# A time-mix layer with its feed-forward on one core: a sum and a root change places, values are split in two, and one half's GELU sums go to TensorE unfolded

## What is computed

```python
xk = x + xx * (time_maa_k + mk)                  # as xw, xv, xr, xg; xx = x_prev - x
r, k, v = xr @ Wr.T, xk @ Wk.T, xv @ Wv.T
g = jax.nn.silu(xg @ Wg.T)
w = time_decay + jnp.tanh(xw @ td_w1) @ td_w2;  decay = jnp.exp(-jnp.exp(w))
def step(S, inp):                                # over time, per head
    kv = k_t[..., :, None] * v_t[..., None, :]
    y = jnp.einsum('bhk,bhkj->bhj', r_t, S + u[None, :, :, None] * kv)
    S = d_t[..., None] * S + kv
...
x = _layernorm(x + attention(x))
h = jnp.einsum('btd,hd->bth', x, absmean(W_fc))  # absmean: weights to -1, 0, 1
h = layernorm(jax.nn.gelu(h, approximate=False), ln_w, ln_b)
x = _layernorm(x + jnp.einsum('bth,dh->btd', h, absmean(W_proj)))
```

## Time and profile before

| | |
|---|---|
| median of 3 runs | 3215.41 us |
| lowest and highest | 3205.75 and 3225.23 us |
| profiled execution, its time | 3207.57 us |
| its span, first to last instruction | 3205.8 us |
| PE busy | 2944.2 us, 92% |
| DVE busy | 2516.8 us, 79% |
| ACT busy | 1978.0 us, 62% |
| POOL busy | 914.2 us, 29% |
| mean granted TensorE clock | 0.981 |

### The profile page before, as it was taken

One profiled execution on the slowest core, in us unless ns is written; L12 is line 12 of the kernel. 1 busy time (PEld: TensorE's weight loads), 2 busy tenths in 40 slices (PEclk: granted clock), 3 DMA queues, 4 the chain that ended last, 5 costly groups with the idle time before them and its releaser, 6 DMA issues.

```text
span 3205.8 us, 101790 instructions
## 1 busy us (share of the span) xinstructions
PE 2944.2 (92%) x40249; PEld 2168.0 (68%) x40249; DVE 2516.8 (79%) x5336; ACT 1978.0 (62%) x4175; POOL 914.2 (29%) x793
## 2 busy tenths in 40 slices
PE   1889999999999999999999999999999999999997
PEld 0666677767676767666766766767666776666765
DVE  8467887777788778788777787777788777788787
ACT  0456667656566666667666666666567655567664
POOL 3223222223322233322232322133322222322132
PEclk9899999999999999999999999999999999999999
DMA  5000000000000000000000000000000000000000
GB/s 206 13 9 22 12 22 19 22 15 22 15 19 19 22 15 22 22 12 21 19 22 15 22 12 19 21 18 19 22 12 22 19 22 15 22 12 22 19 22 14
DMA packets 22822, 73.40 MB, mean 23 GB/s; under 512 B 3104, under 2 KB 3360, under 8 KB 20768
## 3 DMA queue, kind: packets, MB, share of 16 engines
q1 hardware_dynamic: 22432, 67.10, 6.2%
HBM read 50.31 MB, written 16.78 MB: 21 GB/s over the span
## 4 chain that ended last, share of the span: by engine, by line
PE 43%; issue 24%; DVE 14%; POOL 14%; ACT 2%; POOLq 1%; DMA 1%; DVEq 1%; SPq 0%; ACTq 0%
PE psP L404 18%; POOL MT L907 9%; PE psP L442 7%; PE psF L638 5%; PE psF L657 2%; POOL ARENA L921 2%; PE psW L498 2%; DVE ARENA L1220 2%; DVE ARENA L1168 2%; DVE SUMS L1335 2%; DVE HLO L1343 2%; DVE ARENA L1179 2%; PE psW L481 1%; POOL ARENA L943 1%; PE psY L535 1%
## 5 line engine op out<-in xcount | busy, mean ns | idle before, releaser
L404 PE MATMUL psP<-ARENA,WALL 128*128 128x256 f32 x3072 | 732.5, 396 | 66.2 <-POOL ARENA L921 64.8
L687 ACT ACTIVATE ARENA<-ARENA 32x512 f32<-32x512 f32 (+3 forms) x1026 | 584.7, 570 | 225.1 <-DVE ARENA L1168 119.3
L404 PEld LDWEIGHTS psP<-ARENA,WALL 128*128 128x128 f32 x3072 | 596.9, 198 | 154.9 <-ACT ARENA L730 67.4
L1343 DVE SCALAR_TENSOR_TENSOR HLO<-GG,FWB,HHI 128x128 f16<-128x128 f32 x1024 | 350.2, 403 | 319.2 <-ACT HHI L858 314.2
L638 PE MATMUL psF<-XLO,WFC 128*128 128x128 f16 x4096 | 489.8, 220 | 11.0 <-issue 11.0
L638 PE MATMUL psF<-XHI,WFC 128*128 128x128 f16 x4096 | 491.1, 220 | 2.7 <-DVE ST L1361 1.9
L907 POOL TENSOR_TENSOR MT<-ARENA 32x256 fp32r<-32x256 f32 x330 | 318.5, 965 | 500.6 <-ACT ARENA L687 472.0
L638 PEld LDWEIGHTS psF<-XHI,WFC 128*128 128x128 f16 x4096 | 399.2, 98 | 39.5 <-issue 33.8
L638 PEld LDWEIGHTS psF<-XLO,WFC 128*128 128x128 f16 x4096 | 402.4, 98 | 30.7 <-issue 23.0
L921 POOL TENSOR_TENSOR ARENA<-ARENA,XT 128x1024 f32<-128x1024 f32 x128 | 278.2, 2173 | 475.6 <-DVE ARENA L1102 475.6
L657 PE MATMUL psF<-WPJ,HHI 128*128 128x512 f16 x1024 | 389.7, 381 | 13.6 <-ACT GG L849 13.6
(11 more groups left out here) (166 smaller groups left out, 5234.0 us busy)
## 6 DMA issues: line engine op xcount, KB each, us to landing
XT<-x_ch SPq DMA_DIRECT2D x33, 520.0 KB, 3.4
ARENA<-x_tok SPq DMA_DIRECT2D x32, 512.0 KB, 3.7
out<-OUT SPq DMA_DIRECT2D x64, 256.0 KB, 2.1
WALL<-w_all SPq DMA_DIRECT2D x5, 1024.0 KB, 15.3
ARENA<-wfc SPq DMA_DIRECT2D x4, 1024.0 KB, 7.9
ARENA<-wpj SPq DMA_DIRECT2D x3, 1024.0 KB, 14.6
GG<-wpj SPq DMA_DIRECT2D x1, 1024.0 KB, 18.6
OUT<-w2a SPq DMA_DIRECT2D x8, 64.0 KB, 14.0
```

The lines of the kernel that those rows point to most:

```text
L404: mm = pe.matmul(psP[:, P.bank(f"{name}{g}"), COLS * c:COLS * (c + 1)], WALL[:, w, k, 128 * (2 * g + c):128 * (2 * g + c + 1)], cc(XF[slot ...
L687: return act.activation(o, i, ACT.Copy)
L1343: e = dve.scalar_tensor_tensor(out=HLO[:, k, :], in0=GG[:, u % 2, 0, 128 * m:128 * (m + 1)], scalar=FWB[:, 0, k:k + 1], in1=HHI[:, k, :], ...
```

## The change

- The row root of tile `it` leaves the end of POOL's tile and becomes `row_root(it)`, called in the next tile behind the keys' sum; the wait for `mv_ready` goes with it.
- DVE's folds of the first half go. PE sums that half from `SUMS`, four matmuls that accumulate for each of the two sums, in place of one from `GR`. Its wait is on the third addition, and DVE's first addition of the second half waits for PE's sums. The second half is folded as before.
- PE takes `up(1, 2)` between `values(0)` and `values(1)`, not behind both.
- DVE weighs the output before it updates the state.
- In the setup all eight comparisons are DVE's.

```diff
@@ PE, tile
                 values(0)
+                if ffn:
+                    ffn.up(1, 2)
                 values(1)
-                if ffn:
-                    ffn.up(1, 2)
@@ PE, feed_forward
                 def stats(j, p):
-                    pe.wait_ge(sums_folded, 2 * (PAIRS * j + p) + 2)
+                    if p:
+                        pe.wait_ge(sums_folded, 2 * (j + 1))
+                    else:
+                        pe.wait_ge(sums_added, 3 * PAIRS * j + 3)
                     F.wait_free(pe, j, f"st_{p}", first)
                     for i in range(2):
-                        mm = pe.matmul(psF[:, F.bank(f"st_{p}"), i:i + 1], GR[:, i, :], ONES[:, 0:1], start=True, stop=True)
+                        if p:
+                            mm = pe.matmul(psF[:, F.bank(f"st_{p}"), i:i + 1], GR[:, i, :], ONES[:, 0:1], start=True, stop=True)
+                        else:
+                            for m in range(4):
+                                mm = pe.matmul(psF[:, F.bank(f"st_{p}"), i:i + 1], SUMS[:, i, 128 * m:128 * (m + 1)], ONES[:, 0:1],
+                                               start=(m == 0), stop=(m == 3))
@@ POOL
-            pool.wait_ge(setup_step, 9)
-            for n, k in enumerate(POOL_PARTS):
...
                     pool.tensor_tensor(v, v, xcur, ALU.add).then_inc(xf_ready, 1)
+                    if f == 1 and not first:
+                        row_root(it - 1)
...
                 mix_low(it, 2, 10)
-                pool.wait_ge(mv_ready, 2 * (it + 1))
+
+            def row_root(t):
+
+                pool.wait_ge(mv_ready, 2 * (t + 1))
                 inverse_root(RSTD[:, :]).then_inc(rstd_ready, 1)
...
                 def alone():
+                    row_root(j)
@@ DVE, setup
-                if k in POOL_PARTS:
-                    dve.wait_ge(below_ready, POOL_PARTS.index(k) + 1)
-                else:
-                    if k:
-                        dve.wait_ge(quantised, k)
-                    dve.tensor_scalar(BELOW[0], RAW[k], SC[:, 20 + i:21 + i], None, ALU.is_lt).then_inc(setup_step, 1)
...
+                if k:
+                    dve.wait_ge(quantised, k)
+                dve.tensor_scalar(BELOW, RAW[k], SC[:, 20 + i:21 + i], None, ALU.is_lt).then_inc(setup_step, 1)
...
@@ DVE, tile
-                    if ffn and n == 4:
-                        ffn.fold(0, 0)
-                if ffn:
-                    ffn.fold(0, 1)
                 scale_left(5, 32)
...
-                state(0)
-                state(1)
                 dve.wait_ge(y_squared, 2 * it + 2)
...
                 e.then_inc(y_weighed, 1)
+                state(0)
+                state(1)
                 dve.wait_ge(p_full, P.full(it, "var"))
@@ DVE, feed_forward
                     if g == 1:
-                        if p or not first:
-                            dve.wait_ge(sums_folded, 2 * (PAIRS * j + p))
+                        if p:
+                            dve.wait_ge(f_full, F.full(j, "st_0"))
+                        elif not first:
+                            dve.wait_ge(sums_folded, 2 * j)
...
-                        stats(p)
+                        if p:
+                            fold(j, 1, 0)
+                            fold(j, 1, 1)
```

More of the change, by code:

```diff
@@ L187, in rwkv_ffn_kernel @@
         VHI, VLO = sb("VHI", [128, 2, MH], F16), sb("VLO", [128, 2, MH], F16)
-        BELOW = [h[:, :, :].rearrange("p m t -> p (m t)") for h in (HHI, HLO)]
+        BELOW = HHI[:, :, :].rearrange("p m t -> p (m t)")
         PAUSE = sb("PAUSE", [1, 8])
@@ L205, in rwkv_ffn_kernel @@
         raw_in = [sem(f"raw_in{k}") for k in range(8)]
-        below_ready = sem("below_ready")
         xt_in, xtok_in, out_stored = sem("xt_in"), sem("xtok_in"), sem("out_stored")
@@ L266, in rwkv_ffn_kernel @@
         NWEIGHTS = 8 + 5 * 4
-        POOL_PARTS = (2, 5, 7)
         def over_tiles(eng, attention, feed_forward):
@@ L571, in tile @@
                 values(0)
-                values(1)
                 if ffn:
                     ffn.up(1, 2)
+                values(1)
                 pe.wait_ge(y_squared, 2 * it + 2)
@@ L1050, in _ @@
                 part = slice(2048 * (k % 4), 2048 * (k % 4 + 1))
-                if k in POOL_PARTS:
-                    dve.wait_ge(below_ready, POOL_PARTS.index(k) + 1)
-                else:
-                    if k:
-                        dve.wait_ge(quantised, k)
-                    dve.tensor_scalar(BELOW[0], RAW[k], SC[:, 20 + i:21 + i], None, ALU.is_lt).then_inc(setup_step, 1)
-                    n += 1
-                    dve.wait_ge(setup_step, n)
+                if k:
+                    dve.wait_ge(quantised, k)
+                dve.tensor_scalar(BELOW, RAW[k], SC[:, 20 + i:21 + i], None, ALU.is_lt).then_inc(setup_step, 1)
+                n += 1
+                dve.wait_ge(setup_step, n)
                 dve.scalar_tensor_tensor(out=dst[:, :, :].rearrange("p a n -> p (a n)")[:, part], in0=RAW[k],
-                                         scalar=SC[:, 18 + i:19 + i], in1=BELOW[k in POOL_PARTS], op0=ALU.is_gt,
+                                         scalar=SC[:, 18 + i:19 + i], in1=BELOW, op0=ALU.is_gt,
                                          op1=ALU.subtract).then_inc(quantised, 1)
@@ L1351, in fold @@
                     dve.tensor_reduce(GR[:, i, :], SUMS[:, i, :].rearrange("p (m t) -> p t m", m=4), AX.X, ALU.add).then_inc(sums_folded, 1)
-                def stats(p):
-                    fold(j, p, 0)
-                    fold(j, p, 1)
                 def moments(j, p):
@@ L1424, in alone @@
                         stored(j, p)
-                return FeedForward(normalise=normalise, tokens=tokens, up=up, stats=stats, finish=lambda: finish(j, 0), normed=lambda: normed(j, 0),
-                                   stored=lambda: stored(j, 0), late_fold=late_fold, fold=lambda p, i: fold(j, p, i), moments=lambda: late(moments), late=lambda: late(product), late_normed=lambda: late(normed), late_stored=lambda: late(stored), alone=alone)
+                return FeedForward(normalise=normalise, tokens=tokens, up=up, finish=lambda: finish(j, 0), normed=lambda: normed(j, 0),
+                                   stored=lambda: stored(j, 0), late_fold=late_fold, moments=lambda: late(moments), late=lambda: late(product), late_normed=lambda: late(normed), late_stored=lambda: late(stored), alone=alone)
             over_tiles(dve, tile, feed_forward)
```

## The result

The changed kernel takes 3113.7 us (median of four runs, 3113.1 to 3115.3) where the kernel before takes 3210.6 (3190.0 to 3225.2): a ratio of 0.970, 95% interval 0.965 to 0.976. It is faster by 97 us; the forecast was 3138, and its range, 3108 to 3184, holds the time. The sign and the two largest gains, the clock and the stop ahead of k, came out as worked out. The term for the "issue" stops, 24.1 us, came out as 29.8 us, but for a reason that the experiments overturn.

A forecast was written before the change was run, and what follows sets the result against it. PE, the busiest engine, was taken as the bound: a step costs its work plus its stops. Terms summed to -77.1 us from the profiled 3207.6, so 3130.5, scaled to a median of 3138 us; range 3108 to 3184.

The forecast's parts named there:

- the clock: k's first 16 matmuls: after the shorter stop the low clock follows in no step, 21 x 1.68 = 35.3 us won.
- the stop ahead of k: PE's wait for POOL's keys' sum falls from 2.06 to 1.32 us with the sum ahead of the root, 23.9 us won.
- Rival 2: Something else keeps POOL until the root, so the stop ahead of k and the low clock stay: 3197 us; chance 0.06.
- Rival 1: The low clock stays, at k or elsewhere, as with the unfolded sums' one-column loads: up to 35.3 us, 3173; chance 0.20.
- Unfolded sums: 12 more PE records a step lose 41.5 us; dropping DVE's fold wins 23 us at the levels, 7.7 at the transposes.
- Rival 3: The levels don't gain, ACT's copies or DVE's short waits come next; 23 and 7.7 us stay out: 3169; chance 0.07.
- The values' halves: A projection between the halves breaks PE's instruction burst: 18.5 us of issue stops go at line 563, 5.6 at line 638.
- rival 4: Shifted instruction blocks make PE run dry in every step, not ten: slower, 136 us, 3268; chance 0.04.
- State and weighing: DVE weighs while waiting for the values, state follows; x's mix starts about 0.1 us later, 3 us lost at line 657.
- Setup: Comparisons moved from POOL to DVE shorten the selections: 7 us won, bounds 1 to 9.
- The case at the edge: In the setup, POOL's zeroing falls beside a DVE comparison: up to 5.2 us, its length, lost there.
- Tail: One pair of DVE folds (2 us) goes for 1.3 us on PE: 0.6 us won.

The follow-up runs named there:

- e1: Changed kernel with POOL taking the row root ahead of the keys' sum again, as in the old order; 3178.7 us.
- e2: Kernel before with one part of the change alone, POOL's row root behind the keys' sum; 3139.4 us.
- s1: e4 with 12 one-column matmuls and their loads (24 instructions) added in the setup, where PE waits anyway; 3110.7 us.
- e3: Changed kernel with the values' two halves next to each other again on PE, the third up-projection behind them; 3110.5 us.
- e4: Changed kernel with the first half's GELU sums folded by DVE again, 4 records on PE instead of 16; 3128.5 us.
- s3: e4 with 128 one-column matmuls and their loads (256 instructions, one 16 KB block) added in the setup; 3141.7 us.
- r9: Kernel before with the row root behind the keys' sum and 12 one-column matmuls with loads (24 instructions) in the setup; 3114.7 us.
- e5: Changed kernel with DVE's state update ahead of the weighing again, values still in two halves; 3161.4 us.
- e7: Changed kernel with two more ACT exponentials, results unused, ahead of those that free k's bank; 3142.0 us.
- e9: Changed kernel with PE's late down-projection (8 records) moved from ahead of the values' mix to between the second decay product and k; 3085.7 us.
- r10: s1 with PE's late down-projection moved between the second decay product and k, and POOL's zeroing put behind the comparisons; 3079.5 us.

## Why the prediction was right, and where not

- **The stop ahead of k**: right in mechanism and size. ACT frees the bank, 1.22 us remain where 1.32 were forecast (-26.7 instead of -23.9). POOL's sum ends at 1575.88, ACT's exponentials start at 1576.47, as the earlier trace rows let expect: half of them have to pass. Rival 2 (the sum not brought forward) did not occur.
- **The clock**: 35.3 us, as forecast, and by e1 and e2 caused by the stop. Rival 1 did not occur: the 1.8 us of one-column records at a stretch leave the clock at 1.00.
- **Unfolded sums**: the term was 1.34 us a step, it measured 1.21; from the first of 16 records to the next line it takes 1.81 us, four took 0.60, and PE then stood 0.26. The rows of the changed kernel, PE in order of time:

```profile
1630.88 1.95 PE L652 MATMUL psF<-CF,SUMS 128*128 128x1 f32 x16
1632.69 0.63 PE L507 MATMUL psX<-CF,ARENA 128*128 128x128 f32 x4
```

  The 0.75 us stop of the earlier trace rows is gone, the one of 0.42 stays, and the levels give 0.81 a step (0.74 forecast); the 0.26 us of the transposes go as forecast. Net +0.14 where the sum had +0.35; the step of s1 is 0.11 shorter than that of the changed kernel. By the steps the unfolding itself costs about 3 us. Rival 3 did not occur.
- **The values' halves**: the step that failed. "So the 1.57 us go", since a projection breaks the burst, was read from the distance of two stops in one step. e3 shows that the halves bring nothing where the packets lie well. Where they lie badly (e2 against e4) the halves clear line 563 in the loop, but line 638 goes from 10.4 to 17.1 us: some 8 us net (25.9 to 17.7) and not 24.1. The sum had 24.1, the trace 29.8, because the unfolded sums' 24 instructions did it; that the two numbers lie close is luck. This very mechanism stood in the prediction as rival 4, with the one sign that I gave it, slower, and 0.04. Nothing in the earlier trace rows said which way a shift would go; that ten steps already showed the stop spoke for the present place being a bad one, and so for a gain by a shift.
  The Trainium skill, "Runtime: NRT & Kernel Launch", Instruction fetch mechanics, gives the 16 KiB block of 256 instructions, with which s1 and s3 agree, and calls the cost of crossing a block's end "mostly hidden". In this loop it is 25.9 of 3139 us in e2 and 1.8 us with 24 instructions more ahead of it (r9).
- **State and weighing**: 3 us lost were forecast, none are seen (wait of line 663 14.4 us, 13.6 before).
- **Setup**: -3.2 us instead of -7, within its 1 to 9. PE's setup sums start 3.4 us earlier (69.80 to 66.38), and in e1 to e5, e7, e9, s1 and r9 this start is within 0.2 us of the one or the other; the way from there to the first k of tile 1 scatters by some 4 us between executions of one setup (182.8 in e4, 186.8 in the changed kernel; with the old setup 190.0 in the kernel before and 193.4 in r9), for a reason that no run shows, so that 3.2 is one pair out of a spread. The case at the edge came: POOL's zeroing fell beside a comparison. POOL, and DVE's comparison, in the changed kernel:

```profile
46.20 5.22 POOL L880 MEMSET ARENA<- 128x6144 f32 x1 [45.75 <-DVE WFC L1060]
```

```profile
46.18 6.32 DVE L1057 TENSOR_SCALAR HHI<-ARENA,SC 128x2048 f16<-128x2048 f32 x1
```

  The next comparison takes 1.29 us, so this one lost 5.03, about the whole of the zeroing; it ended 1.08 us behind it. The Trainium skill's rule of the port pair locked for a whole instruction ("SBUF — State Buffer", two separate sides) agrees with this pair: by it the comparison would end at some 51.42 + 1.29 = 52.7 us (an estimate), and it ended at 52.50. The selection of the earlier trace rows beside POOL's comparison was 2 us shorter than the rule. All selections are at 2.35 us.
- **Tail**: -0.6 forecast, +3.3 measured; its low clock lasts 19.1 us where it was 14.4, and what that costs is not measured. The tail takes 142 to 147 us in the profiled executions of all these kernels, so most of the 3.3 can be scatter.
- **From the profiled time to the median**: I scaled by 1.0024, 7.5 us. The runs of before lie 35 us apart, the four of the changed kernel 2.2, and there the profiled one is the highest. That the stops and the clock's falls make the spread is likely but not shown: r9, with 1.8 us of the one and none of the other, has 11.4 us. The profiled time itself was the better forecast.

The forecast was 24 us high: 9 by this last step, 6 each by the sums and the issue stops, 3 each by the stop and the weighing, against 8 the other way (setup, tail); some 5 are not assigned.

## What to carry over

Price a stop of TensorE with the clock that may follow it: here shortening 2.06 us to 1.22 gave 0.84 us and, on average, 1.1 more from the clock. Where PE stops "for issue" at the same record in many steps of a loop, shift the loop by a few idle instructions in the setup before restructuring anything: it is one small edit, it tells whether the ends of the packets are the cause, and it was worth 18 to 25 us here. It also means that any edit that changes PE's count of instructions can gain or lose that much for no reason of its own, so an edit's worth is to be read from two kernels with the same stops.

## What the hardware showed

- A block of instructions that ends at a bad place stops PE for 0.65 to 1.57 us in 9 to 16 of 30 steps; 24 instructions further it doesn't, 256 further it does again (17.7, 0 and 17.9 us in e4, s1 and s3).
- The low clock is a matter of how often, not of whether: 0, 9 and 21 to 24 of 31 steps after stops of 1.22, 1.74 and 2.06 us, in the loop all behind stretches in which PE had worked at 2.4 GHz; each costs 1.68 us in k's 16 matmuls.
- fp32 records with one column and a 128x128 load follow each other at 0.11 us (16 in 1.81 us to the next line's start).
- While POOL zeroes 128x6144 (5.22 us), short instructions of DVE take up to that much longer: a comparison 6.32 instead of 1.29 us in the changed kernel, a scaling of 128x64 3.10 instead of 0.19 in r10, where it ends with the zeroing; the reduction between, which began 0.14 us ahead of the zeroing, kept its 2.28 us.
